# Layers 2 and 3 of a Flamingo stack: V projected inside the attention phase, evicted by ScalarE

## The reference

```
Q = LN(x) @ Wq + bq;  K = ctx @ Wk + bk;  V = ctx @ Wv + bv        (split in 16 heads of 8)
sc = Q K^T / sqrt(8);  sc = -inf where mean(|ctx|) <= 0.8           (layer 2 only)
w = nan_to_num(softmax(sc));  o = w V;  x += tanh(g) * (o @ Wo + bo)
```

## Time and profile before

| | |
|---|---|
| median of 3 runs | 5704.32 us (5701.73 to 5706.47) |
| the profiled execution | 5706.84 us, its span 5705.1 us |
| busy over the span | PE 89%, DVE 84%, ACT 54%, POOL 27% |
| mean granted PE clock | 0.93 |
| layer 2, preparation to first max matmul | 3087.7 to 3193.9 us |
| layer 3, the same | 4424.4 to 4522.7 us |

### The profile page before, as it was taken

How to read it: one execution, slowest core, us unless ns; L and a number is a source line. 1 busy time by engine, 2 the same in 40 slices (tenths; PEclk the granted TensorE clock), 3 DMA queues, 4 the chain that set the end, 5 groups by cost and what they waited for, 6 DMA issues and landing times. The chain is left out here.

```text
span 5705.1 us, 74603 instructions
## 1 busy us (share of the span) xinstructions
PE 5058.3 (89%) x26863; PEld 1958.8 (34%) x26872; DVE 4773.0 (84%) x5111; ACT 3066.1 (54%) x5929; POOL 1556.1 (27%) x1168
## 2 busy tenths in 40 slices
PE   8939999999999999999932799999997599999997
PEld 5524444445454544444411222222223122222222
DVE  7459989898989899899868899999982799999993
ACT  3314444444444444444410288888882188888884
POOL 0015556565656565655612000000000200000000
PEclk9969999999999999999965799999995599999996
DMA  0043233333324232322102211111100411111100
GB/s 30 1 131 101 65 94 86 91 87 85 104 67 122 55 115 53 105 70 55 28 4 61 47 21 21 26 21 21 26 7 7 100 21 21 25 22 21 21 16 5
DMA packets 164054, 293.78 MB, mean 51 GB/s; under 512 B 26492, under 2 KB 103752, under 8 KB 160616
## 3 DMA queue, kind: packets, MB, share of 16 engines
q1 hardware_dynamic: 159592, 287.70, 20.4%
q10 hardware_dynamic: 4096, 1.29, 0.1%
HBM read 178.92 MB, written 109.89 MB: 51 GB/s over the span
## 5 line engine op out<-in xcount | busy, mean ns | idle before, releaser
L1599 DVE TENSOR_REDUCE a_mx<-ps 128x1 f32<-128x1024 f32 x1536 | 1820.2, 1220 | 151.4 <-PE ps L1479 129.4
L1566 ACT ACTIVATE a_prob<-ps 128x512 f32<-128x512 f32 (+1 forms) x3264 | 1705.3, 601 | 426.9 <-PE ps L1467 422.2
L1060 ACT ACTIVATE prob<-ps 128x512 f32<-128x512 f32 (+1 forms) x1888 | 975.0, 602 | 1181.9 <-PE ps L945 1181.8
L1163 POOL TENSOR_TENSOR tot_p<-tot_p,prob 128x512 f32<-128x512 f32 (+1 forms) x896 | 1340.4, 1496 | 921.6 <-ACT prob L1060 856.6
L1088 DVE TENSOR_REDUCE mx<-ps 128x1 f32<-128x1024 f32 x896 | 1051.3, 1215 | 152.9 <-PE ps L922 145.1
L1111 DVE TENSOR_TENSOR tot_d<-tot_d,prob 128x512 f32<-128x512 f32 x928 | 1047.8, 1129 | 87.6 <-ACT prob L1060 36.2
L1479 PE MATMUL ps<-a_K,a_Q 51*128 51x512 bf16 (+1 forms) x3328 | 1068.3, 385 | 49.6 <-DMA a_Q<-q_stack_dram 30.3
L1467 PE MATMUL ps<-a_Q,a_K 51*128 51x512 bf16 (+1 forms) x3264 | 1003.8, 389 | 82.8 <-ACT a_prob L1566 76.6
L1503 PE MATMUL ps<-a_prob,a_V 128*9 128x512 f32 x6528 | 953.9, 609 | 10.9 <-ACT a_acc L1550 10.9
L956 PE MATMUL ps<-prob,V 128*64 128x512 f32 (+1 forms) x3776 | 934.0, 605 | 0.0
L944 PE MATMUL ps<-QA,KA 128*128 128x512 f32 (+1 forms) x1888 | 806.4, 427 | 0.0
(11 more groups left out here) (348 smaller groups left out, 3243.4 us busy)
## 6 DMA issues: line engine op xcount, KB each, us to landing
a_K<-k_stack_dram SPq DMA_DIRECT2D x64, 600.4 KB, 5.8
k_hi_dram<-hi_s SPq DMA_DIRECT2D x112, 256.0 KB, 2.0
k_lo_dram<-lo_s SPq DMA_DIRECT2D x112, 256.0 KB, 2.0
KA<-k_hi_dram SPq DMA_DIRECT2D x64, 384.0 KB, 4.3
KA<-k_lo_dram SPq DMA_DIRECT2D x64, 384.0 KB, 5.5
KB<-k_hi_dram SPq DMA_DIRECT2D x64, 384.0 KB, 6.5
k_bf_dram<-bf_s SPq DMA_DIRECT2D x112, 128.0 KB, 1.7
KM<-k_bf_dram SPq DMA_DIRECT2D x32, 448.0 KB, 7.1
```

The lines of the kernel that those rows point to most:

```text
L1060: nc.scalar.activation(prob[0:r, batch % 2, t % BATCH, :], c.banks(n % 3)[0:r, :], ACT.Exp, scale=SCALE).then_inc(exped, 1)
L1163: nc.gpsimd.tensor_tensor(tot_p[0:r, u % 2, :], tot_p[0:r, u % 2, :], p, ALU.add).then_inc(totalled_p, 1)
L1566: nc.scalar.activation(prob[0:r, batch % 2, t % BATCH, :], c.banks(n % 3)[0:r, :], ACT.Exp, scale=SCALE).then_inc(exped, 1)
L1599: nc.vector.tensor_reduce(mx[:, u % 2, j, i % FULL:i % FULL + 1], c.banks(slot(step), 2), AX.X, ALU.max).then_inc(maxed, 1)
```

## The change

The short DVE phase and the V phase are gone, `v_tmp` with them. Their work is spread:

- POOL copies the mask into `keepv` (layer 2) and writes V's ninth column, right after the memset of `keepv` and ahead of the K memsets.
- PE projects groups 0 to 2 ahead of the first max matmul of the main phase, and group m//4+3 after each fourth max matmul (every second step), to group 12 after m = 39. The groups use the ring of three banks and its semaphores `scored` and `exped`; the ring's numbers move up by 13.
- ACT evicts each tile with one activation, ACT.Copy, with `keepv` as scale, ahead of `take_nm(0)`: 51 activations of 128 columns, written in 16 runs of 8.
- `bv` is no longer added to V. In layer 2 DVE widens it, PE multiplies it by Wo, and DVE adds the product to `bo`, times one or zero (`some`: is any context row kept), at the end of the preparation phase. PE waits there for `some_ready` and the last `mask_ready`, DVE for `kept` and `shift_turned`. `bv` is loaded as a column, not broadcast.
- Two small memsets go (`top_set`, layer 3's `bv`), one comes (`ones`).

```diff
+                        pe.wait_ge(some_ready, 1)
+                        pe.wait_ge(mask_ready, len(mask_groups))
+                        nc.tensor.matmul(c.banks(4)[:, 0:D], bv_wide[:], Wo[:], start=True, stop=True)
+                        nc.tensor.matmul(c.banks(5)[:, 0:1], ones[:], some[:], start=True, stop=True
+                                         ).then_inc(shift_turned, 1)
...
+                        dve.wait_ge(kept, 1)
+                        nc.vector.tensor_copy(bv_wide[:], bv[:].to_broadcast([P, P]))
+                        nc.vector.tensor_reduce(some[:], keepv[:], AX.X, ALU.max).then_inc(some_ready, 1)
+                        dve.wait_ge(shift_turned, 1)
+                        link(nc.vector.tensor_scalar(some[:], c.banks(5)[:, 0:1], 0.5, None, ALU.is_gt))
+                        nc.vector.scalar_tensor_tensor(out=bo[:], in0=c.banks(4)[:, 0:D], scalar=some[:], in1=bo[:],
+                                                       op0=ALU.mult, op1=ALU.add)
...
                     link(nc.gpsimd.memset(keepv[:], 0.0 if masked else 1.0))
+                    if masked:
+                        nc.gpsimd.tensor_copy(keepv[:, 0:ST - 1], c.keep[:, 0:ST - 1])
+                        nc.gpsimd.tensor_copy(keepv[0:LAST, ST - 1:ST], c.keep[0:LAST, ST - 1:ST]).then_inc(kept, 1)
+                        pool.wait_ge(kept, 1)
+                    nc.gpsimd.tensor_copy(V[:, :, :, DH], keepv[:].unsqueeze(2).to_broadcast([P, ST, HEADS]))
...
-        with phase(nc, "chain", "unused") as (block, chain, _):
...
-        with phase(nc, "chain", "projected", "v_out") as (block, chain, projected, v_out):
...
         def ring_no(u, t):
-            return 1 + (ST + 1) * u + t + (1 if t >= NM_AT and u + 1 < UNITS else 0)
+            return len(VG) + 1 + (ST + 1) * u + t + (1 if t >= NM_AT and u + 1 < UNITS else 0)
...
+                def project_v(g):
+                    t0, k = VG[g]
+                    if g >= 3:
+                        pe.wait_ge(exped, g - 2)
+                    for j in range(k):
+                        r = rows_of(t0 + j)
+                        last = nc.tensor.matmul(c.banks(g % 3)[0:r, j * D:(j + 1) * D],
+                                                c.ctxT[:, (t0 + j) * P:(t0 + j) * P + r], Wv[:], start=True, stop=True)
+                    last.then_inc(scored, 1)
...
                 ahead = MM + 2 * LEAD
+                for g in range(3):
+                    project_v(g)
                 for m in range(ahead):
                     max_score(m)
+                    if m % 4 == 3 and m // 4 + 3 < len(VG):
+                        project_v(m // 4 + 3)
...
+                for n, (t0, k) in enumerate(VG):
+                    act.wait_ge(scored, n + 1)
+                    for j in range(k):
+                        t, r = t0 + j, rows_of(t0 + j)
+                        last = nc.scalar.activation(
+                            V[0:r, t, :, 0:DH], c.banks(n % 3)[0:r, j * D:(j + 1) * D].rearrange("p (g v) -> p g v", v=DH),
+                            ACT.Copy, scale=keepv[0:r, t:t + 1])
+                    last.then_inc(exped, 1)
                 take_nm(0)
```

More of the change, by code:

```diff
@@ L1215, in narrow_attention @@
         bq, bk = sb("bq", [P, 1]), sb("bk", [P, 1])
-        bv, bo = sb("bv", [P, D]), sb("bo", [P, D])
+        bv, bo = sb("bv", [P, 1]), sb("bo", [P, D])
         K = [sb(f"K{i}", [P, S], BF16) for i in range(2)]
@@ L1219, in narrow_attention @@
         V = sb("V", [P, ST, HEADS, VW])
-        v_tmp = sb("v_tmp", [P, 4, D])
         mx = sb("mx", [P, 2, UQ, FULL + 1])
@@ L1230, in narrow_attention @@
         if bq_in is not None:
-            moves += [(bq[:], bq_in.unsqueeze(1)), (bk[:], bk_in.unsqueeze(1)), (bv[:], bv_in.partition_broadcast(P))]
+            moves += [(bq[:], bq_in.unsqueeze(1)), (bk[:], bk_in.unsqueeze(1)), (bv[:], bv_in.unsqueeze(1))]
         load(c, moves, name)
@@ L1241, in narrow_attention @@
             mask_row = c.sb(f"{name}_mask_row", [1, S], BF16, cut)
-            top_set = c.sb(f"{name}_top", [1, 2], FP32, cut)
+            ones, bv_wide = (c.sb(f"{name}_{n}", [P, P], FP32, cut) for n in ("ones", "bv_wide"))
+            some = c.sb(f"{name}_some", [P, 1], FP32, cut)
             with phase(nc, "bias_set", "projected", "whole_out", "hi_cut", "mid_cut", "cut_done", "stored_0", "stored_1", "stored_2", "top_stored",
-                       "chain", "cleared", "mask_turned", "mask_ready") as (
+                       "chain", "cleared", "mask_turned", "mask_ready", "kept", "some_ready", "shift_turned") as (
                     block, bias_set, projected, whole_out, hi_cut, mid_cut, cut_done, stored_0, stored_1,
-                    stored_2, top_stored, chain, cleared, mask_turned, mask_ready):
+                    stored_2, top_stored, chain, cleared, mask_turned, mask_ready, kept, some_ready, shift_turned):
                 stored = (stored_0, stored_1, stored_2)
@@ L1407, in ring_no @@
         def ring_no(u, t):
-            return 1 + (ST + 1) * u + t + (1 if t >= NM_AT and u + 1 < UNITS else 0)
+            return len(VG) + 1 + (ST + 1) * u + t + (1 if t >= NM_AT and u + 1 < UNITS else 0)
         def nm_no(u):
-            return 0 if u == 0 else 1 + (ST + 1) * (u - 1) + NM_AT
+            return len(VG) + (0 if u == 0 else 1 + (ST + 1) * (u - 1) + NM_AT)
         def step_at(i):
@@ L1464, in score @@
                         pe.wait_ge(exped, nm_no(u) + 1)
-                    if n >= 3:
-                        pe.wait_ge(exped, n - 2)
+                    pe.wait_ge(exped, n - 2)
                     nc.tensor.matmul(c.banks(n % 3)[0:r, :], K[(u // HALVES) % 2][0:ROWS, t * P:t * P + r],
```

4 lines of the change are left out of this document (2 added, 2 removed).

## The result

| | before | after |
|---|---|---|
| median | 5705.13 us (5701.73 to 5711.74, 10 runs) | 5689.34 us (5670.79 to 5691.61, 10 runs) |
| profiled execution, its span | 5706.84, 5705.1 us | 5689.39, 5687.6 us |
| ratio, 95% interval | | 0.9967 (0.9958 to 0.9976) |

The change gains 15.8 us. The forecast was 46. I cut the two traces at the same instructions: the first POOL memset of the preparation, the first K load, the first reduction, the copy of the first offset into Q, that of the second, that of the last, and the update of x. Each entry is a difference of starts, in us.

The account below looks back on a forecast made before the run. It took serial DVE work to bound the head of layers 2 and 3; -50.23 + 1.4 + 1.0 + 2 x 1.0 = -45.8 us gave 5661.0 from the profiled 5706.84, or 5658.5 from the median, range 5650 to 5667.

Parts of the forecast that it names:

- What bounds the kernel: Head of layers 2 and 3: serial DVE work of 25 us, and a lead-in bound by DVE, 33.89 of 35.20 us busy.
- what is removed: Short DVE phase: the first K load issues 25.47 us earlier in layer 2, 24.76 in layer 3, together 50.23 us.
- POOL: Preparation: the new column copy, taken as 1.0 us, delays the K memsets; layer 2 +1.4 us, layer 3 +1.0.
- The bias: Layer 2, end of preparation: the new chain takes 2.5 us at most, hidden behind SP's loads and waits of 5.3 us.
- ACT: Lead-in: evicting four V tiles takes 1.1 us per group of 2.27 us or more, hidden behind DVE.
- PE in the lead-in: V groups among max matmuls: clock expected to rise within two pairs of steps, +1.0 us a layer; ends -1.0 and +10.6.
- rival (b): Lead-in: the clock never rises, 10.6 us a layer instead of 1.0, giving 5677.7 us; chance 9%.
- The range: Forecast's own range, 5650 to 5667 us: below, lead-ins -1.0; above, POOL at 2.4 and 2 us worse a layer.
- The loop: Main loop: work unchanged, the clock expected low again at its start, nothing won.
- (a): Rival: full clock reached in the lead-in lasts into the main loop, about 3.3 us a layer, so 5652; chance 13%.

Follow-up runs that it names:

- e6: Against e5, POOL writes V's ninth column after the four K memsets instead of ahead of them; 5657.92 us.
- e2: Changed kernel plus eight 128-row filler matmuls, result unread, between V group 2 and the first max matmul; 5662.04 us.
- e5: Changed kernel with five V groups instead of three ahead of the first max matmul; 5657.69 us.
- e3: Changed kernel with the first unit's max matmuls reading all 128 rows instead of 51, so its results differ; 5667.62 us.
- e4: Changed kernel; from the second pair of steps on, the first unit's two max matmuls per step use two row blocks, 0 to 50 and 64 to 114; 5666.09 us.
- e1: Changed kernel with V groups 3 to 12 projecting one tile of four, the rest of V left out; 5663.92 us.
- e8: e5 with each K tile's constant rows set by one memset of 32-bit words instead of two of 16-bit elements; 5631.47 us.
- e9: As e2, but the eight filler matmuls use 51 rows instead of 128; 5674.96 us.
- e10: e8 plus the two row blocks of e4 and four filler matmuls per pair of steps after the last V group; 5629.75 us.
- e11: e8 plus four filler matmuls per pair of steps after the last V group, without two row blocks; median 5632.7 us, runs 5611.08 to 5641.65.

## Why the prediction was wrong

**What bounds the kernel, what is removed: right.** SP and DVE start the main phase where the short DVE phase stood. The preparation with its V phases lost 24.11 and 23.72 us; the terms -25.47 + 1.4 and -24.76 + 1.0 make 24.07 and 23.76. That the two agree within 0.04 us is luck: over the traces with this same work the stretch moves by 1.2 us in layer 2 and 0.65 in layer 3. The K load to the first reduction kept its length (8.0 and 8.6 us).

**POOL: right in the sum, for another reason.** The copy is 1.64 us, not 1.0: the row of a contiguous copy was too low for this form, and DVE's 1.60 for the form itself the better one. It delays the K memsets by 1.9 us in layer 2 and 1.5 in layer 3, and 1.4 and 1.0 arrive. By e6 this is no matter of what stands ahead of the memsets.

**The bias, ACT: right.** The chain is over 3.6 us before the phase is. ACT's tile is 368 ns on average, 1.14 us for four; it waits for PE.

**PE in the lead-in: the step that failed.** The forecast said that a PE-bound lead-in has no gaps, "so I expect the rise within two pairs". From 3175 it has no gaps for 36 us, and the clock stayed at 0.50. That groups 0 to 2 raise the clock came true, and helped for one pair only. The row that I took it from the earlier trace rows is V groups alone, 128 rows at every matmul; the lead-in mixes them with max matmuls of 51 rows. Layer 0, the other witness, enters warm before, and its max matmuls have 128 rows (`128*128` in the row itself): I read the time off it and not the shape. The last row of the same group, the loop's end at PE 5.00 and 0.50, was in front of me as the argument for rival (b), at 9%. e2 and e5 hold the clock by work ahead of the first step, e3 and e4 raise it by the rows, at once or in two blocks. The +1.0 a layer was +13.2 and +13.9.

**Rival (b), too cheap.** It priced ten pairs at 3.40 - 2.35, 1.06 us. Each pair also pays 0.45 us for the switches between 51 and 128 rows (3.82 against 3.37 in e3): 1.47 a pair. From the profiled execution the forecast was 5661.0; with +13.2 and +13.9 in place of +1.0 each it is 5661.0 + 25.1 = 5686.1. Of the 3.3 us left to 5689.39, 3.0 are in layers 0 and 1 and 1.1 at the loops' ends, less 0.8 in the first stretches.

**The range.** Its own ends do not quite follow from the terms named: both lead-ins at -1.0 give 5658.5 - 4.0 = 5654.5, not 5650, and POOL at 2.4 with 2 us more a layer 5658.5 + 2.8 + 4.0 = 5665.3, not 5667. Neither difference matters to the outcome, which lies beyond even rival (b)'s 5677.7.

**The loop: right, and (a) did not happen.** The first stretch starts at the low clock in the changed kernel, in e1 to e6, e8 and e9. It takes fillers to change it, and they give 1.2 to 2.2 us a layer (e10 and e11 against e5), less than (a)'s 3.3. With the lead-in warm (e5) the time is 5657.7, the forecast 5658.5: the sum was that of a kernel which keeps PE at work ahead of the first step. The 0.8 us are in part luck, since e5's lead-ins are 0.3 us shorter than before, not 1.0 longer.

## What to carry to other kernels

Ask of a phase that moves onto TensorE at which clock it will be entered and what PE does just before, not only how busy it will be; price it at the low clock, with its own shapes, and make the doubtful case the forecast unless a row with the same mix shows the rise. A wait of two microseconds just ahead of a long thin stretch can cost more than the wait: put needed work there first. A wait that is left behind more work (1.46 us in e5) cost nothing. And look at memsets of narrow, 16-bit tiles when another engine stretches beside them; here 17 us of them a layer cost 14 on the path.

## What the runs showed of the hardware

- With V groups (128 rows) and max matmuls (51 rows) in turn the granted clock kept either level: 1.00 for 20 us and more, to behind the last group (e2, e5, both layers), or 0.50 for 36 us with PE busy throughout, once it had fallen (the kernel after, layer 2; e9's layer 3 alike). With 128 rows throughout, or two blocks of 51 at once, it rose from 0.50 within two to three pairs (e3 and e4, both layers; layer 0 of the kernel after).
- It fell after a wait of 1.86 us that began as it rose (the kernel after), and did not after one of 1.46 us that came 2.9 us after the rise (e5, layer 3).
- The Trainium skill (TensorE: Matmul & The Clock Gate, "What's actually happening") says that the clock follows how busy the PE has been. By the profile's busy time alone this case does not follow it: PE is busy 5.00 of 5.00 us in both e3, where the clock rises, and the kernel after, where it does not. What the chip counts these runs don't tell.
- Alternating matmuls of 51 and 128 rows cost 0.45 us per turn and back at 1.2 GHz: a pair takes 3.82 us in the kernel after, 3.37 with 128 rows throughout (e3).
- The same code, PE's scores and weighing beside ACT's exponential, took 50 us at the end of a loop where the clock held (e11, layer 2) and 65 to 69 us where it fell.
- Beside POOL's memsets DVE's casts are held: a cast of 0.43 us takes 3.00 and 4.89 beside memsets of 5.6 us, 2.28 and 2.22 beside memsets of 2.9 us (e8).
